# A recurrent block with adaptive normalization: the gates' shift rows from 16 stationary columns, two gates moved together

## What is computed

```python
h = LN(x) * (1 + ca) + sa
x = x + ga * attn(h)          # h_t = tanh(h_{t-1} @ A.T + x_t @ B.T); y_t = h_t @ C.T; then LN(y + x)
h = LN(x) * (1 + cb) + sb
# ffn: a gated recurrence over the 8 batches, xt = h[b], a matrix of 1024 x 256; its state c starts at in_c
ft = sigmoid(xt @ wf.T + c @ uf.T + bf)
it = sigmoid(xt @ wi.T + c @ ui.T + bi)
gt = tanh(xt @ wc.T + c @ uc.T + bc)
c  = ft * c + it * gt
x  = x + gb * tanh(h @ wo.T + c_final @ uo.T + bo)
```

## Time and profile before

| what | us |
| --- | --- |
| median of 3 executions | 560.26 |
| lowest, highest | 559.84, 561.21 |
| span of the profiled execution, first to last instruction | 558.3 |
| PE busy | 542.1 (97%) |
| PE's loads busy | 531.2 (95%) |
| DVE busy | 394.1 (71%) |
| ACT busy | 341.0 (61%) |
| POOL busy | 344.1 (62%) |

### The profile page before, as it was taken

One profiled execution on the slowest core, in us unless ns is written; L12 is line 12 of the kernel. 1 busy time (PEld: TensorE's weight loads), 2 busy tenths in 40 slices (PEclk: granted clock), 3 DMA queues, 4 the chain that ended last, 5 costly groups with the idle time before them and its releaser, 6 DMA issues.

```text
span 558.3 us, 13427 instructions
## 1 busy us (share of the span) xinstructions
PE 542.1 (97%) x4620; PEld 531.2 (95%) x4620; DVE 394.1 (71%) x908; ACT 341.0 (61%) x862; POOL 344.1 (62%) x475
## 2 busy tenths in 40 slices
PE   6999999999999999999999999999999999999994
PEld 3899999999999999999999999999999999999983
DVE  5998878886767665555866676776667676686663
ACT  3777777785466555465765556666665566667651
POOL 4767777660376444454776666677666757778454
PEclk9999999999999999999999999999999999999998
DMA  8666445434243222222133333443333333323244
GB/s 274 181 189 197 146 151 152 127 103 154 85 139 108 72 72 75 78 68 77 57 105 103 103 103 94 120 124 107 96 95 96 95 96 103 123 78 114 67 114 153
DMA packets 58514, 64.10 MB, mean 115 GB/s; under 512 B 5408, under 2 KB 49736, under 8 KB 58448
## 3 DMA queue, kind: packets, MB, share of 16 engines
q1 hardware_dynamic: 58448, 63.26, 37.2%
HBM read 46.44 MB, written 16.81 MB: 113 GB/s over the span
## 4 chain that ended last, share of the span: by engine, by line
PE 76%; POOL 7%; issue 6%; ACT 4%; DVE 3%; DMA 2%; SPq 1%; POOLq 0%; DVEq 0%; ACTq 0%
PE psI L1578 11%; PE psOF L1578 11%; PE psG L1578 11%; PE psWR L1537 6%; PE psWR L1636 6%; PE psWR L1449 4%; PE psWR L1484 4%; PE psOF L1484 4%; PE psOF L1449 4%; PE psC L1564 3%; PE psOF L1564 3%; PE psT L1615 2%; POOL wx L705 2%; ACT xn L851 1%; PE psC L1501 1%
## 5 line engine op out<-in xcount | busy, mean ns | idle before, releaser
L649 POOL TENSOR_TENSOR hin<-hin,uvec 128x256 f32<-128x256 f32 x64 | 50.9, 816 | 32.5 <-ACT hin L813 30.1
L656 POOL TENSOR_TENSOR hsl<-hs,hsh 128x512 fp32r<-128x512 f32 x24 | 30.9, 1289 | 49.1 <-DVE state L1304 32.6
L1285 DVE SCALAR_TENSOR_TENSOR lo<-psT,cb1T,hi 128x256 fp32r<-128x256 f32 x60 | 26.2, 478 | 41.8 <-ACT hi L878 41.8
L690 POOL TENSOR_TENSOR zn<-zn,tA 128x512 f32<-128x512 f32 x32 | 46.1, 1440 | 11.0 <-ACT zn L851 11.0
L1150 DVE TENSOR_TENSOR pre<-psWR,state 128x256 f32<-128x256 f32 x44 | 18.5, 420 | 46.1 <-PE psWR L1537 45.8
L851 ACT ACTIVATE zn<-state,nmA,rstdA 128x256 f32<-128x256 f32 x64 | 35.0, 594 | 26.1 <-POOL nmA L680 26.1
L1537 PE MATMUL psWR<-hs,AT 128*128 128x128 f32 x368 | 49.5, 274 | 0.0
L663 POOL TENSOR_TENSOR xin<-xin,tA 128x512 f32<-128x512 f32 x32 | 41.3, 1289 | 13.3 <-DMA tA<-rows_d 13.3
L840 ACT ACTIVATE hs<-pre 128x256 f32<-128x256 f32 x44 | 18.4, 417 | 50.7 <-DVE pre L1150 50.5
L1104 DVE SCALAR_TENSOR_TENSOR hin<-xin,mvA,uvec 128x256 f32<-128x256 f32 x56 | 41.4, 777 | 9.5 <-DMA h_park<-hin 9.0
L1537 PEld LDWEIGHTS psWR<-hs,AT 128*128 128x128 f32 x368 | 45.2, 191 | 0.1
(11 more groups left out here) (384 smaller groups left out, 2313.4 us busy)
## 6 DMA issues: line engine op xcount, KB each, us to landing
h_park<-hin SPq DMA_DIRECT2D x32, 256.0 KB, 2.2
hin<-h_park SPq DMA_DIRECT2D x64, 128.0 KB
xin<-in_L_attn_x_dram SPq DMA_DIRECT2D x64, 128.0 KB
tA<-rows_d SPq DMA_DIRECT2D x32, 256.0 KB, 4.4
out_dram<-state SPq DMA_DIRECT2D x64, 128.0 KB
xin<-in_L_attn_x_dram SPq DMA_DIRECT2D x28, 256.0 KB, 2.8
tW<-rows_d SPq DMA_DIRECT2D x32, 128.0 KB, 3.2
tG<-rows_d SPq DMA_DIRECT2D x24, 128.0 KB, 3.6
```

The lines of the kernel that those rows point to most:

```text
L649: pool.tensor_tensor(h, h, sa, ALU.add).then_inc(a_h, 1)
L690: pool.tensor_tensor(two(zn[:, :]), two(zn[:, :]), both(tA[:, m % 2, 0:D]), ALU.mult).then_inc(s_zg, 1)
```

## The change

The few stationary columns get their high and low parts side by side: sbT_hl and c0z_hl are 128 x 2 x 16, and one instruction with 16 stationary columns gives the high part's product in partitions 0 to 7 and the low part's in 8 to 15. The high weights go through once for both. A second instruction with the 8 high columns adds the low weights' product into partitions 0 to 7. The weights of gates f and i are kept in one tensor each for w and u (high and low), so that both gates move as 512 columns in one instruction. The two halves (partitions 0 to 7 and 8 to 15) are summed where rows become columns: instead of a transpose against an 8 x 8 identity, a matmul against fold, a 16 x 8 matrix of two identities, one over the other. fold is made by one DVE add behind the five small operations.

In place of three blocks of 12 instructions of 256 columns there are a block of 8 of 512 columns (gates f and i, unit 7, where shift_row(0) was) and a block of 8 of 256 columns (gate c, unit 8, where shift_row(1) was); the place of shift_row(2) is empty. ACT's first copy waits for a count lower by one.

```diff
+        phi = {n: sb(n + "fiT_hi", [P, 2, H, D], f32r) for n in PAIRED}
+        plo = {n: sb(n + "fiT_lo", [P, 2, H, D], f32r) for n in PAIRED}
+        sbT_hl = sb("sbT_hl", [P, H, 2, NB], f32r)
+        c0z_hl = sb("c0z_hl", [P, H, 2, NB], f32r)
+        fold = sb("fold", [2 * NB, NB])
...
-                    for i, src in enumerate((psW[0:NB, :], psI[0:NB, 0:D])):
-                        act.wait_ge(q_gb, 3 + i)
+                    for i, src in enumerate((psW[0:2 * NB, :], psI[0:2 * NB, 0:D])):
+                        act.wait_ge(q_gb, 2 + i)
...
+                dve.tensor_tensor(fold[:, :], ident[0:2 * NB, 0:NB], ident[0:2 * NB, NB:2 * NB], ALU.add).then_inc(q_sbc, 1)
...
-                pe.wait_ge(q_sbc, 5)
+                pe.wait_ge(q_sbc, 6)
...
-            def shift_row(i):
-
-                ps = (psW[0:NB, 0:D], psW[0:NB, D:W], psI[0:NB, 0:D])[i]
-                n = 0
-                for name, shi, slo in ((("wf", "wi", "wc")[i], sbT_hi, sbT_lo), (("uf", "ui", "uc")[i], c0z_hi, c0z_lo)):
-                    for k in range(H):
-                        for w, few in ((whi, shi), (whi, slo), (wlo, shi)):
-                            n += 1
-                            last = pe.matmul(ps, few[:, k, :], w[name][:, k, :], start=(n == 1), stop=(n == 12))
+            def shift_rows(ps, given):
+
+                for i, (few, high, low) in enumerate(given):
+                    for k in range(H):
+                        pe.matmul(ps[0:2 * NB], few[:, k, :, :].rearrange("p s b -> p (s b)"), high[k],
+                                  start=(i == 0 and k == 0), stop=False, skip_group_check=True)
+                    for k in range(H):
+                        last = pe.matmul(ps[0:NB], few[:, k, 0, :], low[k], start=False, stop=(i == 1 and k == H - 1),
+                                         skip_group_check=True)
                 last.then_inc(q_gb, 1)
 
+            def shift_rows_fi():
+                shift_rows(psW, [(few, [phi[w][:, :, k, :] for k in range(H)], [plo[w][:, :, k, :] for k in range(H)])
+                                 for few, w in ((sbT_hl, "w"), (c0z_hl, "u"))])
+
+            def shift_rows_c():
+                shift_rows(psI[:, 0:D], [(few, [whi[w][:, k, :] for k in range(H)], [wlo[w][:, k, :] for k in range(H)])
+                                         for few, w in ((sbT_hl, "wc"), (c0z_hl, "uc"))])
...
-                        last = pe.transpose(psI[:, at:at + NB], shr[:, i, m * P:(m + 1) * P], ident[0:NB, 0:NB])
+                        last = pe.matmul(psI[:, at:at + NB], shr[:, i, m * P:(m + 1) * P], fold[:, :], start=True, stop=True)
...
                 if u == ML:
                     project(here[1])
-                    shift_row(1)
+                    shift_rows_c()
...
                     pe.wait_ge(s_tanh, 4 * AP)
-                    shift_row(0)
+                    shift_rows_fi()
                 if u == ML:
-                    shift_row(2)
                     project(here[2])
```

## The result

| what (five executions each) | before | after |
| --- | --- | --- |
| median, us | 560.26 | 571.18 |
| lowest, highest, us | 559.79, 561.21 | 569.95, 572.80 |
| span of the profiled execution, us | 558.3 | 571.0 |

The ratio is 1.0206, 95% interval 1.0192 to 1.0219: by the medians 10.9 us slower, where 1.15 us were forecast and 562.2 was the upper end of the range. The profiled execution after took 572.76 us.

A forecast was written before the change was run, and what follows sets the result against it. PE, full from 170 to 310 us, was taken to enter late by the path from project(c2) through DVE, POOL and ACT. +0.40 + 0.89 - 0.12 = +1.17, say +1.15, on span 558.3, plus 1.96 to the median: 561.4 us, range 560.0 to 562.2.

The forecast's parts named there:

- Edits with one answer: Small edits costed at nothing, among them DVE's add for fold, some 0.1 us, hidden by 1.49 us of idle DVE.
- whatever PE is late by at 170 us stays to the end: PE works 140.00 of 140.00 us from 170 to 310 us, so delay on entry carries to the end.
- rival (e): Holes at step(19) and tokens(0) let the clock fall to 1.2 GHz over tokens(0) to the gates: 564 us, chance 0.03.
- The block of f and i: Unit 7, ahead of project(c2): 8 instructions of 512 columns take 1.76 us for 1.36, +0.40 us.
- rival (c): Unit 7: a wide fp32r matmul costs little more than a narrow one, 560.6 us, chance 0.05.
- The 1.81 us less in unit 8: Less PE work for gates i and c, costed at nothing: it becomes holes at step(19) and tokens(0).
- shift_columns: Unit 9, between tokens(0) and step(20): six transposes become ordinary matmuls with 12 records, 1.35 us for 0.46, +0.89 us.
- Rival (b): In shift_columns, ordinary matmuls of 8 columns cost about as the transposes: 560.5 us, chance 0.14.
- (d): Between tokens(0) and step(20), shift_columns costs more still, 2.4 us at the upper bound: 562.5 us, chance 0.13.
- Given back at step(20): Behind shift_columns: step(20)'s wait for the tanh of step(19) goes when PE is later, -0.12 us.
- (a): PE is the path all along up to tokens(0), and its work counts: -0.5 us, 559.7 us, chance 0.05.
- (f): Unit 7: a wide instruction is issued as two of 256 columns, 1.81 us for 1.76; no chance given.

The follow-up runs named there:

- e1: The kernel before with one unused 32-byte tile per partition ahead of state, no instruction changed: 568.55 us, ratio 1.0139.
- e16: The changed kernel with fold lying in 256 bytes a partition instead of 32, at the same place: 563.11 us, ratio 1.0047 against the kernel before.
- e2: The changed kernel with fold declared behind all other tiles, so state and later tiles stand as before the change: 561.75 us, ratio 1.0023 against the kernel before.
- e14: The kernel before with only shift_columns changed, to six ordinary f32 matmuls against the 8 x 8 identity instead of transposes: 560.99 us, ratio 1.0015.
- e13: The changed kernel without fold, f and i block moved to unit 8 behind project(c3), 16-column transposes, halves summed on DVE: 558.58 us, ratio 0.9974 against before.
- e8: The changed kernel, layout kept, with 8 unused matmuls ahead of step(19) and 6 ahead of tokens(0): 570.23 us, ratio 1.0175 against the kernel before.
- e5: The kernel before with B's weights 64 bytes further into the tiles shared with chi and clo, each tile 128 bytes longer: 563.15 us, ratio 1.0054.
- e9: The kernel before with chi and clo 32 bytes further and what is declared behind clo 128 bytes further: 565.64 us, ratio 1.0092.
- e10: The changed kernel with fold declared ahead of the weights, so weights and state both move 32 bytes: 562.29 us, ratio 1.0038 against the kernel before.

## Why the prediction was wrong

**The step that failed** stands under "Edits with one answer". It costs the DVE add that fills fold and finds cover for it; the tile itself has no line, and so the price nothing. Its 32 bytes move the moving operands of 2117 gate matmuls against their weights. Price by two pairs of runs: 7.9 us on the kernel before (e1), 8.1 us on the change (after against e16; these two differ also in the clock, whose fall shows in four of five executions of after and in three of six of e16). Behind it stands an assumption that was not argued: "whatever PE is late by at 170 us stays to the end", and the full stretch from 170 to 310 us adds nothing of its own. I read from that row that PE sets the time there, and then did not ask whether the change touches the pace of its instructions. Where an engine works 140.00 of 140.00 us, 4 ns on an instruction is worth more than any microsecond ahead of the stretch.

**The clock**, rival (e), was given 0.03. Its price was about right (1.7 by the spans to 2.1 us by the medians within e16; forecast 564 against 561.4, so 2.6), its chance was not. The earlier trace rows showed full clock through a longer idle time, and I took that as a bound for shorter holes; it wasn't one. Four of the five executions of after have a mean clock of 0.993, the fifth 0.995.

**The sum** of the terms that were costed was right in total: +1.15 forecast, +1.13 measured (e2; by its interval 0.7 to 1.8). That it agrees to 0.02 us is luck: three terms are each off by about 0.1 the same way. Term by term, from distances of starts:
- The block of f and i: 139.65 to 141.51, 1.86 us where 1.76 were forecast and 1.81 was the upper bound; a wide matmul costs 233 ns, over twice a narrow one, and the fixed part that the forecast took off isn't there; rival (c) is out. +0.50 for +0.40.
- The 1.81 us less in unit 8 gave nothing, as forecast, and turned into two holes, 0.74 and 0.71 us (forecast 1.3 and 0.6).
- shift_columns: 154.11 to 155.54, 1.43 us for 0.46, x12, 119 ns a record where 110 were forecast. +0.97 for +0.89. Rival (b), cheap records, and (d), 157 ns and more, are out.
- Given back at step(20): nothing, where -0.12 was forecast. From its start to project(c6) it is 0.91 us in e14 (154.00 to 154.91) and 0.91 in the kernel before; the longer duration in the earlier trace rows is only that of the modelled ends.
That makes +1.47 by the rows; the medians give 0.34 less, within their interval.

**The rivals.** (a), PE's own work alone as the path, is out: 1.3 us less work gave holes (after, e2); only with 1.36 us moved from in front of project(c2) as well did it give a gain, 1.55 us (e13). (f) is not seen: a wide matmul is one record.

**Adding up**: 1.1 us (own terms, e2), 7.9 (place of the operands, e1), and for the clock 1.0 (after against e8) to 2.1 (within e16) make 10.0 to 11.1; measured 10.9.

The sign that was to tell, "PE's busy time is down by 0.5 to 1 us", was the first to show it: up by 12.0 instead. PE's wait between 170 and 310 us, named there as a sign of being wrong, did come, 0.32 us at tokens(2); but it is the wait of 0.34 us that stood at 169.49 before, moved into that stretch.

## What to carry to other kernels

Where one engine is full for most of the span, read the price of each of its instructions as something that an edit can change from afar: a new buffer, however small, moves all that is declared behind it, so put it last (e2) or, in a layout like this one, give it 256 bytes (e16), and compare the distance of starts in a block that the edit doesn't touch. Taking work off a full engine gained nothing here until the chain that feeds it started earlier; move work behind the head of that chain, and look whether the holes that a shorter program leaves cost the clock.

## What the hardware showed that I had not expected

- The same matmul (fp32r, 128 x 128 stationary, 256 moving columns) costs 113 to 120 ns by where its two operands lie to each other in a partition: 114.1, 118.2, 119.9, 117.1, 116.1 and 118.7 ns with 0, 32, 64, 96, 128 and 192 more bytes between them, and 114.2 again with 256. The best and the worst are 13.6 us of 560 apart. The Trainium skill, TensorE: Matmul & The Clock Gate, section Step-by-step: what each phase is for, says that the moving operand and the weight load have read ports of their own, so that loading the next weights takes no read bandwidth from the running matmul. These runs show that the pace depends on how the two operands lie to each other; by what mechanism, and why 128 and 192 bytes cost what they do, stays open, and so does why chi slowed in e5 along with clo, and times_wo in e9 behind the slow blocks.
- In after, holes of 0.74 and 0.71 us with a block of 12 small records behind them were followed by the clock at 1.2 GHz (0.50 from 157 to 159 us in after). In the profiled execution of e2 the same holes were not followed by it, and by the mean clock neither were half of e16's and eight of e10's ten. What decides was not settled.
- 512 moving columns in fp32r, against 8 or 16 stationary ones, cost 233 ns. The Trainium skill, TensorE: Matmul & The Clock Gate, section Back-to-back issue gap, gives 131 ns for a stream of load and matmul pairs of that width; the measurement decides, and by it a wide instruction saves nothing over two narrow ones of 113 ns.
